# Output projection of a gated attention block from half-precision high and low parts, three products for one

## The reference, cut to what matters

```python
out = jnp.einsum('bhij,bhjd->bhid', attn, v)
out = out.transpose(0, 2, 1, 3).reshape(b, m, h * d)
return out @ Wout + bout
...
x = x + jnp.tanh(g_xattn[0]) * _L0_xattn_ref(...)
x = x + jnp.tanh(g_ffn[0]) * _L0_ffn_ref(_layernorm(x, axis=-1), ...)
```

## Time and profile before

| what | value |
|---|---|
| device time, median of 3 runs | 379.69 us (377.49 to 379.92) |
| device time of the profiled execution | 380.09 us, of which its span 378.3 us |
| TensorE busy | 319.7 us, 85% of the span |
| VectorE busy | 289.8 us, 77% |
| ScalarE busy | 194.4 us, 51% |
| GpSimd busy | 255.3 us, 67% |
| L1141, float32 projection products, 128 records | 275 ns median of one |
| L1124, transposes of the pieces, 64 records | 273 ns median of one |
| L630, copy of a turned piece, 16 | 586 ns median |
| L946, row maxima, 64 | 1222 ns mean |
| L519, low half of an exponential on GpSimd, 64 | 1900 ns mean |

### The profile page before, as it was taken

How to read it: one execution, slowest core, us unless ns; L and a number is a source line. 1 busy time by engine, 2 the same in 40 slices (tenths; PEclk the granted TensorE clock), 3 DMA queues, 4 the chain that set the end, 5 groups by cost and what they waited for, 6 DMA issues and landing times.

```text
span 378.3 us, 9354 instructions
## 1 busy us (share of the span) xinstructions
PE 319.7 (85%) x3618; PEld 196.8 (52%) x3641; DVE 289.8 (77%) x578; ACT 194.4 (51%) x329; POOL 255.3 (67%) x197
## 2 busy tenths in 40 slices
PE   1644745879999999999999999999998798769993
PEld 0122422326556555555566555777876575535562
DVE  4874564778888889898898885874726988889994
ACT  2532326554565655565565645655682547235551
POOL 7694458478888888797898897746763426326652
PEclk9966576699999999999999999999999999989997
DMA  6307000350260440620701607543000000001001
GB/s 186 103 15 152 2 9 1 74 103 3 38 138 8 95 84 6 138 41 3 170 11 26 149 7 196 102 116 107 3 0 2 2 2 0 3 0 29 0 3 29
DMA packets 31470, 20.38 MB, mean 54 GB/s; under 512 B 11650, under 2 KB 30914, under 8 KB 31426
## 3 DMA queue, kind: packets, MB, share of 16 engines
q1 hardware_dynamic: 30482, 19.75, 23.0%
q10 hardware_dynamic: 944, 0.04, 0.2%
HBM read 5.87 MB, written 0.52 MB: 17 GB/s over the span
## 4 chain that ended last, share of the span: by engine, by line
POOL 29%; issue 27%; PE 24%; DVE 12%; ACT 5%; DMA 1%; POOLq 1%; DVEq 0%; ACTq 0%
POOL p_lo L519 15%; POOL p_lo L563 7%; POOL rms_r L442 3%; PE pj L1141 3%; PE tv L1177 2%; PE big L1248 2%; PE big L1249 2%; PE tv L1124 1%; PE o_ps L1164 1%; POOL pc_lo L525 1%; DVE sumsq L824 1%; PE o_ps L1165 1%; DVE qk L834 1%; PE o_ps L1170 1%; POOL v L537 1%
## 5 line engine op out<-in xcount | busy, mean ns | idle before, releaser
L519 POOL TENSOR_TENSOR p_lo<-p 128x1024 f16<-128x1024 f32 x64 | 120.6, 1900 | 21.0 <-ACT p L660 20.9
L660 ACT ACTIVATE p<-big 128x1024 f32<-128x1024 f32 x64 | 65.6, 1025 | 61.3 <-PE big L1249 59.2
L946 DVE TENSOR_REDUCE nm_main<-big 128x2 f32<-128x1024 f32 x64 | 78.2, 1222 | 16.7 <-PE big L1189 16.2
L442 POOL TENSOR_TENSOR rms_r<-meansq,power 128x8 f32<-128x8 f32 x32 | 52.3, 1638 | 29.2 <-DVE meansq L828 28.5
L563 POOL TENSOR_TENSOR p_lo<-p,p_lo 128x512 f16<-128x512 f32 x32 | 37.1, 1160 | 47.1 <-ACT p_lo L738 44.8
L1248 PE MATMUL big<-w 128*128 128x512 f16 x128 | 48.9, 382 | 1.4 <-ACT p L660 1.4
L1249 PE MATMUL big<-w 68*128 68x512 f16 x128 | 48.7, 380 | 0.0
L1164 PEld LDWEIGHTS o_ps<-v,p 128*128 128x128 bf16 x512 | 35.9, 99 | 9.4 <-issue 4.1
L1164 PE MATMUL o_ps<-v,p 128*128 128x65 f16 x512 | 40.7, 194 | 0.0
L1165 PE MATMUL o_ps<-v,p 128*128 128x64 f16 x512 | 40.6, 195 | 0.0
L1165 PEld LDWEIGHTS o_ps<-v,p 128*128 128x128 bf16 x512 | 34.4, 98 | 5.5 <-issue 0.3
(11 more groups left out here) (206 smaller groups left out, 778.2 us busy)
## 6 DMA issues: line engine op xcount, KB each, us to landing
w<-hl SPq DMA_DIRECT2D x64, 128.0 KB, 3.5
w<-hl SPq DMA_DIRECT2D x16, 256.0 KB, 4.1
hl<-n_kernel_gating_EDF_dram SPq DMA_DIRECT2D x1, 1024.0 KB, 6.3
hl<-L_ffn_kernel_up_EDF_dram SPq DMA_DIRECT2D x1, 1024.0 KB, 5.7
o_sb<-in_L_xattn_Wkv_dram SPq DMA_DIRECT2D x2, 384.0 KB, 7.1
x_sb<-in_x_dram SPq DMA_DIRECT2D x2, 256.0 KB, 4.4
wout<-in_L_xattn_Wout_dram SPq DMA_DIRECT2D x1, 512.0 KB, 5.0
k1c<-kc_hl SPq DMA_DIRECT2D x32, 8.0 KB, 1.8
```

The source lines that it names most:

```text
L442: nc.gpsimd.tensor_tensor(rms_r[:, tau % QT, :], meansq[:, tau % QT, :], power[:, 0:8], ALU.pow).then_inc(rr_ok, 1)
L519: nc.gpsimd.tensor_tensor(p_lo[m % NP][:, :], p[m % NP][:, :], p_hi[m % NP], ALU.subtract).then_inc(plo_ok, 1)
L660: nc.scalar.activation(p[n % NP][:, :], st_ps, ACT.Exp).then_inc(exp_ok, 1)
L946: nc.vector.tensor_reduce(nm_main[:, u % 2, 2 * c:2 * c + 2, q], s2_ps.rearrange("p (k n) -> p k n", k=2), AX_X, ALU.max, negate=True).the ...
```

## The change

Two new tiles hold the high part of the output weights as float16 and the low part as bfloat16. In slot 48 ScalarE writes the high part of all 1024 columns in one copy and VectorE the low part in one subtraction. A turned piece is kept in two halves of the place where it lay as float32: ScalarE's `evacuate` writes float16, and a new VectorE step `turned_lo(i)` subtracts it from what stands in `tv` and writes the low half as float16. `project_o` makes three products for each one before. `turn_o` and `project_o`, and the turns of the second norm's rows, which reuse `tv`, now wait for `turned_lo` (`oTl_ok`) instead of the copy (`oTa_ok`).

```diff
+        def o_parts(j):
+            parts = o_half(j).bitcast(F16)
+            return parts[:, 0:HALF], parts[:, HALF:2 * HALF]
...
             def evacuate(i):
                 j = O_ORDER[i]
                 act.wait_ge(oT_mm, i + 1)
-                nc.scalar.copy(o_half(j), turned_o()).then_inc(oTa_ok, 1)
+                nc.scalar.copy(o_parts(j)[0], turned_o()).then_inc(oTa_ok, 1)
...
+                if n == 48:
+                    act.wait_ge(rest_in, 16 * 3)
+                    nc.scalar.copy(wout_hi[:, :, :], wout[:, :, :]).then_inc(wohi_ok, 1)
...
+            def turned_lo(i):
+                hi, lo = o_parts(O_ORDER[i])
+                dve.wait_ge(oTa_ok, i + 1)
+                nc.vector.tensor_tensor(lo, turned_o(), hi, ALU.subtract).then_inc(oTl_ok, 1)
...
+                if n == 48:
+                    dve.wait_ge(wohi_ok, 1)
+                    nc.vector.tensor_tensor(wout_lo[:, :, :], wout[:, :, :], wout_hi[:, :, :], ALU.subtract).then_inc(wolo_ok, 1)
+                if n in TURN_AT:
+                    turned_lo(TURN_AT[n])
                 if n - 1 in SPLIT_AT:
                     i = SPLIT_AT[n - 1]
                     dve.wait_ge(wsp_hi, i + 1)
...
                     nc.vector.tensor_tensor(h, h, scores[n % 2][:, 512:1024], ALU.mult).then_inc(hid_ok, 1)
+                if n in TURN_X:
+                    turned_lo(TURN_X[n])
...
             def project_o(i):
...
-                pe.wait_ge(oTa_ok, i + 1)
+                pe.wait_ge(oTl_ok, i + 1)
...
-                    last = nc.tensor.matmul(y_bank(t), o_half(j)[:, c * P:(c + 1) * P], wout[:, h * (H // 4) + c, :],
-                                            start=(h == 0 and c == 0 and t <= QT), stop=(h == 1 and c == H // 4 - 1),
-                                            skip_group_check=True)
+                    cols, w = slice(c * P, (c + 1) * P), h * (H // 4) + c
+                    nc.tensor.matmul(y_bank(t), hi[:, cols], wout_hi[:, w, :], start=(h == 0 and c == 0 and t <= QT),
+                                     stop=False, skip_group_check=True)
+                    nc.tensor.matmul(y_bank(t), hi[:, cols], wout_lo[:, w, :], start=False, stop=False, skip_group_check=True)
+                    last = nc.tensor.matmul(y_bank(t), lo[:, cols], wout_hi[:, w, :], start=False,
+                                            stop=(h == 1 and c == H // 4 - 1), skip_group_check=True)
```

More of the change, by code:

```diff
@@ L81, in flamingo_gated_block @@
         wout = sb("wout", [P, H // 2, D], F32)
+        wout_hi = sb("wout_hi", [P, H // 2, D], F16)
+        wout_lo = sb("wout_lo", [P, H // 2, D], BF16)
         wr = sb("wr", [P, E], F32)
@@ L185, in flamingo_gated_block @@
         gate_ok, z2b_ok = sem("gate_ok"), sem("z2b_ok")
+        oTl_ok, wohi_ok, wolo_ok = sem("oTl_ok"), sem("wohi_ok"), sem("wolo_ok")
         z2_ok, z2T_ok, x2T_ok, x2hi_ok, x2lo_ok, logit_ok = (sem(n) for n in (
@@ L1114, in turn_o @@
                 else:
-                    pe.wait_ge(oTa_ok, i)
+                    pe.wait_ge(oTl_ok, i)
                 if i == 2 * QT:
@@ L1129, in project_o @@
                 t, h = j // 2, j % 2
-                pe.wait_ge(oTa_ok, i + 1)
+                pe.wait_ge(oTl_ok, i + 1)
                 if i == 0:
-                    pe.wait_ge(rest_in, 16 * 3)
+                    pe.wait_ge(wolo_ok, 1)
                     pe.wait_ge(norm_ok, QT * UNITS)
@@ L1138, in project_o @@
                     pe.wait_ge(x1_ok, QT)
+                hi, lo = o_parts(j)
                 for c in range(H // 4):
-                    last = nc.tensor.matmul(y_bank(t), o_half(j)[:, c * P:(c + 1) * P], wout[:, h * (H // 4) + c, :],
-                                            start=(h == 0 and c == 0 and t <= QT), stop=(h == 1 and c == H // 4 - 1),
-                                            skip_group_check=True)
+                    cols, w = slice(c * P, (c + 1) * P), h * (H // 4) + c
[4 more added lines that the diff above has]
+                                            stop=(h == 1 and c == H // 4 - 1), skip_group_check=True)
                 last.then_inc(y_mm, 1)
@@ L1351, in slot @@
                 if n == NORM_AT + 2:
-                    pe.wait_ge(oTa_ok, 3 * QT)
+                    pe.wait_ge(oTl_ok, 3 * QT)
                     turn_rows2(0)
@@ L1406, in expert_slot @@
                 if n == ROWS_X:
-                    pe.wait_ge(oTa_ok, 2 * T)
+                    pe.wait_ge(oTl_ok, 2 * T)
                     turn_rows2(1)
```

## The result

The changed kernel takes 399.73 us, median of 6 runs (399.24 to 400.74), against 379.14 (377.49 to 379.92, 6 runs) for the kernel before: ratio 1.0574, 95% interval 1.0546 to 1.0602. It is 20.6 us slower. The prediction had the direction, the race and the waits and gave 12.2; the measured time lies 5.2 us above the end of its range, 394.5.

The account below looks back on a forecast made before the run. TensorE was taken as the bound from 237 to 286 us. Waits of 13.0 less 3.3 saved gave 9.7 in attention, plus 2.5 in the expert stage: 12.2 on 379.69, so 391.9 us, range 384.5 to 394.5.

Parts of the forecast that it names:

- the race: Slots 52, 54, 56, 58: VectorE's residual sum starts 0.05 us behind a GpSimd instruction and is held until after its end.
- the waits: Slots 52 to 54, 56, 58: TensorE waits for VectorE's late residual or head, 13.0 us in sum.
- T: The moment when TensorE has issued the transposes of a slot; 253.68 in slot 54 of the kernel before.
- loss over win: Residual's sum at T + 2.36 against GpSimd's T + 2.31: loss taken; rival of all four won, 385.4 us, chance 0.20.
- The product term: Attention projections: twelve half-precision products take 0.67 us instead of 0.98, 0.30 saved each, 11 x 0.30 = 3.3 us.
- more than forecast: Rival: GpSimd's later start also hits L1038, or VectorE's slot 48 backlog reaches slot 52; over 394.5 us, chance 0.05.
- The expert stage: Pieces 12 to 15: `turned_lo` comes late on a nearly full VectorE, 2.5 us longer, bounds 1.2 and 3.9.
- the upper bound of 3.9: Expert stage: 3.9 us if one of the four residual sums there is held for another GpSimd instruction.
- The slot 48 splits: Two weight splits, about 1.05 us on ScalarE and 1.2 on VectorE, covered by nine us of room; priced at nothing.

Follow-up runs that it names:

- kernel with no low half: Changed kernel without the step `turned_lo`, the third product taking the high half again; 375.98 us, ratio 0.9930 to the kernel before.
- The filler: Changed kernel plus twelve unused 128x512 products on TensorE before the awaited step of slots 54, 56 and 58; 394.28 us, ratio 1.0423.
- the two kernels with all pieces halved: Changed kernel with bias added on TensorE and the sum reading PSUM, 383.53 us; the same with batch 0 residuals one slot earlier, 380.18 us.
- the kernel with the late expert piece: Changed kernel with VectorE's low half of an expert piece moved behind the next slot's residual and head; 384.79 us, ratio 1.0178.

## Why the prediction was wrong: the race and the waits right, the clock priced at nothing

**The race, right.** GpSimd at T + 2.31 and the residual's sum at T + 2.36 was the forecast. With T at 255.51 in slot 54 it was 2.31 and 2.35. The step that I took, loss over win by 0.05 us, was measured as 0.04, in three slots out of four. (By the forecast's own terms, 2.04 + 0.33, it is 2.37 and the step 0.06.) The sign of so small a step was luck: it was no wider than the gaps added up, as the forecast said.

**The product term, right.** 0.67 us for a projection, 0.30 saved; 0.29 to 0.30 in slots 55, 57 and 59 of the kernel with no low half. In slots 52 and 56, two of the eleven counted, TensorE only arrives earlier at the head and waits longer.

**The waits, right.** Forecast 2.9, 2.9, 3.4, 2.8 and 1.0 us for slots 54, 58, 56, 52 and 53, sum 13.0. Measured, less what was waited there before: 2.72, 2.79, 3.8 - 0.47 = 3.3, 3.51 - 0.69 = 2.8 and 0.30, sum 11.9. Only slot 53 was off: TensorE came late to it itself, at half clock behind slot 52's wait, so there was less left to wait for.

**The step that failed** is the sum: "Sum of waits 5.8 + 3.4 + 2.8 + 1.0 = 13.0; less 3.3 saved, attention is 9.7 us longer." It prices a wait of TensorE at its length. The waits less the saving are 8.6 us in the trace, and attention grew by 16.4, so 7.8 us are not the waits: the forecast had the clock at nothing. The filler gave 5.6 of them back in three slots by keeping the clock. In slot 52, which had no filler, the same way of reckoning gives 5.01 - 0.30 + 2.8 = 7.5 us where 8.95 was measured, 1.4 more, and the clock is 0.53 there. That makes 7.0 of 7.8.

The granted clock gives the same amount by another way. From the end of each of the four waits to a moment when the clock was back, TensorE was busy all but without a gap, so what the lower level takes is the length times what the clock lacks of 1.00, an estimate:

| slot of the wait | stretch, us | length | granted clock | taken, us |
|---|---|---|---|---|
| 52 | 248.22 to 253.00 | 4.78 | 0.64 | 1.72 |
| 54 | 260.01 to 267.00 | 6.99 | 0.58 | 2.94 |
| 56 | 272.56 to 278.00 | 5.44 | 0.69 | 1.69 |
| 58 | 283.49 to 288.00 | 4.51 | 0.68 | 1.44 |

The sum is 7.8, all of what was missing, and the order is that of the filler's gains (2.74, 1.59 and 1.23 for slots 54, 56 and 58). A wait cost more the longer the low level lasted behind it, not the longer the wait was.

The busy-time rows should have warned me: they show 1.00 for a TensorE that is never idle for long, and say nothing of one that is. Other rows of the same trace did. Behind a wait of 2.19 us in the expert stage of the kernel before, the clock is half for three us:

```profile
335.07 0.23 PE L1386 MATMUL o_ps<-wd_hi,p_lo 128*128 128x128 f16 x1 [2.19 <-POOL p_lo L563]
```
```profile
336.00:339.00 3.00, 2.68 (x11) 0.96 (x10) 2.86 (x9) 0.60 (x1) 0.60 (x1) 0.50 0.00 0
```

The Trainium skill (TensorE: Matmul & The Clock Gate, HAM oscillation — how this bites in real kernels) describes a kernel whose waits for transfers between groups of products put TensorE back to the lower clock each time. The trace agrees, with 0.50 to 0.56 behind waits of 2.7 to 3.8 us. I had not drawn on it, and my rival *more than forecast* named VectorE's backlog and not this.

**The expert stage, 4.8 instead of 2.5,** has three parts; their sizes are in part argued, since the kernels compared differ in more than one thing. First the one I costed: with the residual that reads PSUM, the two kernels with all pieces halved take 47.42 us there, 2.3 more than before; I had 2.5. (They also have the bias's products and no L878; of the four steps alone 1.9 was measured above.) Second, the hold that I had only as the upper bound of 3.9, for which the forecast shows no working. It came true in the residual of token tile 5, with another GpSimd instruction (L572, at 321.34) than in attention:

```profile
321.42 1.22 DVE L879 SCALAR_TENSOR_TENSOR x_sb<-x_t,gates_t,x_sb 128x128 f32<-128x128 f32 x1
...
322.79 0.22 PE L1167 MATMUL pj<-wout_hi,o_sb 128*128 128x128 f16 x1 [2.01 <-DVE x_sb L879]
```

The filler kernel has this hold and a clock of 1.00 up to the last 1.7 us of the stage, and takes 48.60, 1.2 more. Third, the clock again. The changed kernel, the filler kernel and the kernel with the late expert piece have the same two waits in this stage, 2.2 us for L893 and 2.0 for L879, and their stages take 49.98, 48.60 and 51.39 us. What tells them apart in the profiles is the granted clock. The stretches that hold these waits, of the changed kernel, the filler kernel and the late one:

```profile
310.00:330.00 20.00, 15.68 (x150) 10.73 (x149) 17.53 (x41) 7.20 (x14) 5.78 (x5) 0.91 0.00 1
```
```profile
310.00:330.00 20.00, 17.20 (x171) 11.58 (x171) 18.38 (x44) 8.90 (x19) 8.41 (x9) 1.00 0.01 2
```
```profile
290.00:310.00 20.00, 13.97 (x119) 9.86 (x120) 16.11 (x39) 7.81 (x15) 5.79 (x5) 0.89 0.00 1
310.00:330.00 20.00, 19.02 (x162) 11.86 (x161) 16.35 (x39) 10.67 (x22) 8.42 (x10) 0.94 0.01 2
```

In the changed kernel the clock is low behind the second wait only (323 to 327 us), in the late one behind both (298 to 302 and 308 to 312), which fits its longer stage.

So 2.3 + 1.2 + 1.4 (49.98 less 48.60) = 4.9 for the 4.8 measured. Why waits of 2.0 and 2.2 us drop the clock in one kernel and not in another is open: no run here tells what decides it.

**The slot 48 splits** were priced at nothing. They took 1.04 us on ScalarE and 2.08 on VectorE (I had 1.2, plus 1.1 if GpSimd held it, which it did), and no wait of TensorE followed from them.

**The sum again, with the missing term:** waits 11.9, saving -3.3, clock 7.8, expert 4.8, together 21.2; the profiled span grew by 19.1, the difference being the -1.7 and -0.4 of the two ends in the table above.

## What to carry to other kernels

An added step on an engine with spare time is priced by what stands behind it in that engine's order and by what that work then meets, not by its duration alone: here sixteen steps of 0.68 us cost 20 us, and with one neighbour moved out from between it and the residual it cost 6. When a wait of several us on TensorE comes out of such a sum, add the time in which the work behind it runs at half clock, about 1.2 to 2.7 us a wait here; keep new waits short, and move a step by half a us where it starts beside a GpSimd instruction. Before optimising the products, measure the ceiling with the new step left out: it was 0.7% here, too little to pay for any new wait.

## What was not expected of the hardware

- After waits of 2.7 to 3.8 us TensorE's granted clock was 0.50 to 0.56 and came back to 1.00 within some us; after waits of up to 1.9 us between slots 49 and 61 it stayed 1.00. Waits of 2.0 to 2.2 us were seen with both outcomes, and later in the expert stage the clock fell with no wait above 1.7 us in the 35 us before (kernel without the low half, 0.50 from 328 to 333 us). So the length of one wait does not settle it.
- Products with no use, 2.75 us of them in each of three waits, made the program 5.5 us faster.
- 0.04 us of lateness behind GpSimd cost 1.65 us, the same way in three slots of one execution. With one operand in PSUM there is no hold: the gated sum took 0.35 us when it started 0.86 us behind a running GpSimd instruction, and L893 took 0.69 each of the five times that it did.
- Two products over a single row (1x128) ahead of a projection added 0.32 us to a slot, where twelve of 128 rows took 0.67. No run tells whether the row count costs this or the change from one shape to the other.
